# A conv block on one core: the map's 3x3 convolution by a minimal algorithm F(4,3), with its rows staged in fours

## The reference, cut to what matters

```python
x = x + layer(group_norm(x))               # 32 groups
# layer(v):
res = conv3x3(v, W_id, b_id)               # all 8 images
cA, cH, cV, cD = swt2_level3(v[0])         # image 0: circular 8-tap filters,
                                           # dilations 1, 2, 4, rows and columns
low_att  = attention(cA, ...)              # 1x1 conv times a sigmoid scale per channel
high_att = attention(concat(cH, cV, cD))   # 64 -> 192 channels
dmt = concat([low_att, high_att])          # 256 channels
out = leaky_relu(conv3x3(dmt, W_enc, b_enc), 0.01)   # one image: "the map", for all 8
return out + res
```

## Time and profile before

| | us |
|---|---|
| median of 3 runs | 2208.15 (2202.99 to 2209.74) |
| the profiled execution: its time | 2206.73 |
| its span (first to last instruction) | 2204.9 |
| busy: PE / DVE / POOL / ACT | 2132.9 / 1435.6 / 878.9 / 823.5 |
| granted clock of PE, mean | 0.98 |

### The profile page before, as it was taken

One profiled execution on the slowest core, in us unless ns is written; L12 is line 12 of the kernel. 1 busy time (PEld: TensorE's weight loads), 2 busy tenths in 40 slices (PEclk: granted clock), 3 DMA queues, 4 the chain that ended last, 5 costly groups with the idle time before them and its releaser, 6 DMA issues.

```text
span 2204.9 us, 74566 instructions
## 1 busy us (share of the span) xinstructions
PE 2132.9 (97%) x33526; PEld 1521.1 (69%) x33526; DVE 1435.6 (65%) x2235; ACT 823.5 (37%) x765; POOL 878.9 (40%) x543
## 2 busy tenths in 40 slices
PE   8997799999999999997999999999999999999998
PEld 7894566666666666664767776677677876677776
DVE  6755455555555555522777777777777777777776
ACT  3432333333333333322344344344444443444442
POOL 0001544444444444510444444444444444444444
PEclk9987899999999999998999999999999999999999
DMA  7942777777777777603687787887888878878874
GB/s 182 307 148 84 193 166 162 166 164 164 166 164 164 165 163 163 139 2 83 172 202 196 201 208 196 203 206 199 206 206 200 205 200 206 203 197 205 206 196 141
DMA packets 109191, 391.38 MB, mean 178 GB/s; under 512 B 45513, under 2 KB 46056, under 8 KB 95144
## 3 DMA queue, kind: packets, MB, share of 16 engines
q1 hardware_dynamic: 108904, 386.89, 70.3%
HBM read 258.37 MB, written 128.45 MB: 175 GB/s over the span
## 4 chain that ended last, share of the span: by engine, by line
issue 30%; POOL 23%; POOLq 1%; DVE 0%; PE 0%
POOL stage L1172 23%; POOLq L1170 1%; PE ps L1151 0%; POOLq L1165 0%; DVE dev L1107 0%; DVE gsum L1111 0%; DVE quad L1101 0%; DVE gsum L1104 0%; DVE dev L1110 0%; DVE dev L1109 0%; DVE quad L1103 0%; DVE gvar L1112 0%; DVE gmean L1105 0%; POOL root L1164 0%; POOLq L1163 0%
## 5 line engine op out<-in xcount | busy, mean ns | idle before, releaser
L1172 POOL TENSOR_TENSOR stage<-stage,big 128x448 f32<-128x448 f32 x448 | 511.1, 1141 | 661.5 <-DVE stage L1078 661.5
L1078 DVE SCALAR_TENSOR_TENSOR stage<-ps,w_max,xs 64x448 f32<-64x448 f32 x832 | 568.2, 683 | 79.3 <-PE ps L1146 55.0
L1146 PE MATMUL ps<-x_hi,w_hi 64*64 64x448 f16 x8064 | 454.0, 351 | 18.2 <-issue 18.0
L1036 ACT ACTIVATE x_hi<-xs,norm_now 128x2240 f16<-128x2240 f32 x104 | 234.9, 2258 | 608.5 <-PE ps L1146 605.8
L1146 PE MATMUL ps<-x_hi,w_lo 64*64 64x448 f16 x8064 | 451.0, 350 | 0.1
L1146 PEld LDWEIGHTS ps<-x_hi,w_hi 64*64 64x64 f16 x8064 | 294.8, 107 | 125.0 <-issue 23.5
L1146 PEld LDWEIGHTS ps<-x_hi,w_lo 64*64 64x64 f16 x8064 | 294.6, 107 | 106.0 <-issue 3.4
L810 PE MATMUL ps<-d_odd,shared 128*64 128x448 f16 x3024 | 293.5, 353 | 0.0
L810 PE MATMUL ps<-pool_of,shared 128*64 128x448 f16 x3024 | 293.5, 353 | 0.0
L916 DVE SCALAR_TENSOR_TENSOR big<-ps,e_max,lin 128x448 f32<-128x448 f32 x56 | 38.3, 683 | 331.0 <-ACT lin L869 331.0
L810 PEld LDWEIGHTS ps<-d_odd,shared 128*64 128x64 f16 x3024 | 172.4, 109 | 114.6
(11 more groups left out here) (176 smaller groups left out, 1739.7 us busy)
## 6 DMA issues: line engine op xcount, KB each, us to landing
xs<-in_x SPq DMA_DIRECT2D x200, 560.0 KB, 7.1
out<-stage SPq DMA_DIRECT2D x448, 224.0 KB, 3.1
big<-in_x SPq DMA_DIRECT2D x196, 448.0 KB, 7.4
row_filtered<-big SPq DMA_DIRECT2D x4, 6272.0 KB, 21.4
pool_of<-row_filtered SPq DMA_DIRECT2D x54, 448.0 KB, 9.9
pool_of<-in_x SPq DMA_DIRECT2D x32, 392.0 KB, 6.7
big<-in_x SPq DMA_DIRECT2D x8, 560.0 KB, 7.3
xs<-in_x SPq DMA_DIRECT2D x8, 504.0 KB, 7.3
```

What stands on the lines that cost most here:

```text
L1036: act.activation(x_hi[p][:, :, 1:1 + W], xs[slot][:, :].rearrange("p (r w) -> p r w", w=W), ACT.Identity, scale=scale, bias=bias).then_inc ...
L1078: dve.scalar_tensor_tensor(stage[p][o, r, g, :], psum[4 * p + 2 * g + r][o, 0:NT], w_max[lanes, 0:1], xs[slot][lanes, c:c + NT], ALU.mult, ...
L1146: mm = pe.matmul(psum[4 * p + 2 * g + r][C * k:C * k + C, 0:NT], w[lanes, t, :], v[lanes, y:y + 2, kx:kx + W], start=(j == 0), stop=(j == ...
L1172: pool.tensor_tensor(stage[p][:, r, g, :], stage[p][:, r, g, :], e_map[:, e:e + NT], ALU.add)\
```

## The change

The map's convolution is computed along a row by the minimal algorithm F(4,3): four neighbouring outputs need six products (at the points 0, 0.75, -0.75, 1.5, -1.5 and infinity) instead of twelve. The input transform is linear along the row, so it is multiplied into the column filter's matrices `fw`: a generated tile now holds for each of 56 groups of four columns six transformed values (2 x 336 = 672 columns instead of 448, in two PSUM banks). The weights are transformed on DVE. The output transform is made of sums and scalings of the six products on DVE, POOL and ACT, and the leaky ReLU is now x + relu(99 x), the result scaled. Rows come in fours: 56 loads of 4 rows instead of 28 of 8.

PE's tiles and convolution:

```diff
-                    if tile >= 4:
-                        pe.wait_ge(lo_done, tile - 3)
-                    for wc in (1, 0):            # 9 matmuls: 322, 126, 196 columns, 3 each
-                        ...
+                    if tile >= 2:
+                        pe.wait_ge(lo_done, tile - 1)
+                    for sw in range(2):          # 9 matmuls each: 246, 90, 168 columns
+                        o = psum[2 * (tile % 2) + sw][:, 0:VW]
+                        ...
+                    for place, i in enumerate(pair):      # pair of products
+                        o = [psum[bank][C*s:C*s+C, MN*place:MN*place+MN] for s in range(2)]   # MN = 224
+                        pieces = [(a, b, sw, ky) ...]     # 3 * 2 * 3 = 18
+                        for k, (a, b, sw, ky) in enumerate(pieces):
+                            for s in range(2):
+                                r = 4 * s + ky
+                                pe.matmul(o[s], weff[a][:, sw, i, ky, :],
+                                          d[n][:, b, r:r + 4, sw, NTILE*i:NTILE*i+NTILE], ...)
+                        if biased: ...                    # products 0, 1, 2, 5: two more
                 for step in range(NE):
                     for k in range(fresh(step)):
+                        u = 2 * step + 2 + k // CH
+                        if k % CH == 0:
+                            pe.wait_ge(s_split, u - 1)
+                        gen(tile_of(step, k), s_hl[u % 2][:, :, k % CH, :, :])
...
+                    conv(step, 5, (1, 2))
+                    conv(step, 6, (3, 4)).then_inc(conv_done, 1)
+                    if step:
+                        pe.wait_ge(z_done, step)
+                    conv(step, 4, (0, 5)).then_inc(conv_done, 1)
```

SP (load(u) waits for s_split of u - 3, that is until the rows before last are split):

```diff
-                for step in range(NE):
-                    u = step + 2
-                    ...
-                        load(u)
-                    for k in range(CPS * step, min(CPS * step + CPS, NCK)):
-                        load_stats(k)
+                for k in range(2):
+                    load_stats(k)
+                for step in range(NE):
+                    for u in (2 * step + 4, 2 * step + 5):
+                        if u < NU:
+                            load(u)
+                    for k in range(CPS * step + 2, min(CPS * step + 2 + CPS, NCK)):
+                        load_stats(k)
```

DVE in a step (stat(j) is one statistics instruction, four are a chunk):

```diff
+                    now = 16 * (step - 1)
                     for k in range(fresh(step)):
                         lo(tile_of(step, k), m, 2 + k)
-                    for q in range(2): ...        # take_stats twice, then the max
+                        if step and k % 2 == 1:
+                            stat(now)
+                            now += 1
+                        if step and k == 4:
+                            outer(step - 1)       # z0, z3 += products 0, 5
+                    while step and now < 16 * step:
+                        stat(now)
+                        now += 1
+                    pairs(step)                   # sums and differences of products 1 to 4
```

POOL and ACT in a step:

```diff
+                for step in range(NE):            # POOL
+                    if step:
+                        inner(step - 1)           # four additions of 224 elements
+                    for u in (2 * step + 4, 2 * step + 5):
+                        if u < NU:
+                            normal_rows(u)        # waits for the rows' DMA
+                        if step and u % 2 == 0:
+                            leaky(step - 1)       # one addition of 896 elements
+                    for u in (2 * step + 4, 2 * step + 5):
+                        if u < NU:
+                            split_lo(u)
...
+                    if step:                      # ACT
+                        act.wait_ge(conv_done, 2 * step)
+                        scale(step - 1)           # three copies of 224 elements
+                    for k in range(fresh(step)):
+                        hi(tile_of(step, k), m, 2 + k)
+                        if step and k == 5:
+                            positive(step - 1)    # relu(99 z), 896 elements
...                                               # the carried rows, now 2688 elements
+                    split_hi(2 * step + 4)
+                    put(step - 1)                 # waits for leaky; four of 224 elements
+                    split_hi(2 * step + 5)
+                    copy_second(step)             # products 2 and 4, before pairs
```

```diff
                 for k in range(FIRST):            # ACT
                     hi(k, 0, 1 + k)
-                split_hi(1)
+                    if k == 1:
+                        act.activation(weff[0]..., u32..., ACT.Identity, scale=einv[:, 0:1])
+                    if k == 5:
+                        split_hi(2)
+                split_hi(3)
...
+                    if k == 1:                    # DVE, behind lo(1)
+                        dve.wait_ge(weights_high, 1)
+                        dve.scalar_tensor_tensor(weff[1]..., u32..., einv[:, 0:1], weff[0]..., ...)
...
+                pool.wait_ge(weights_ready, 1)    # POOL
+                for u in (2, 3):
+                    normal_rows(u)
+                    split_lo(u)
```

More of the change, by code:

```diff
@@ L747, in tile_of, with rows_of, part_of, z_of @@
             return FIRST + ER * step + k
+        def rows_of(u):
+            return CH - 1 if u == NU - 1 else CH
+        def part_of(n):
+            v = e_map[:, n * EN:(n + 1) * EN] if n < NE else early[:, (n - NE) * EN:(n - NE + 1) * EN]
+            return v.rearrange("p (k n) -> p k n", k=4)
+        def z_of(step):
+            return part_of(step + 2)
+        def side_of(step):
+            return part_of(step + 3)
+        LATE = (ROWS - 2 * SX) // EN
         with nc.Block() as block:
@@ new lines, in gen, with add_bias @@
+                    mm.then_inc(gen_done, 1)
+                def add_bias(o, i, row):
+                    j, v = (0, 1, 2, None, None, 3)[i], 1 if i == NI - 1 else 0
+                    parts = [(0, 1, 0), (1, 4, 1)] if row == 0 else [(0, 3, 1), (3, 4, 2)] if row == H - 4 else [(0, 4, 1)]
+                    for a, b, kind in parts:
+                        m = inside[:, kind:kind + 1, v, :].broadcast_to((P, b - a, NTILE))
+                        mm = pe.matmul(o[:, a * NTILE:b * NTILE], bw[:, j, :], m, start=False, stop=(b == 4))
+                    return mm
@@ new lines, in conv @@
+                def conv(step, bank, pair):
+                    n = step % 2
+                    for place, i in enumerate(pair):
+                        o = [psum[bank][C * s:C * s + C, MN * place:MN * place + MN] for s in range(2)]
+                        pieces = [(a, b, sw, ky) for a, b in ((0, 0), (0, 1), (1, 0)) for sw in range(2) for ky in range(3)]
+                        biased = i not in (3, 4)
+                        for k, (a, b, sw, ky) in enumerate(pieces):
+                            for s in range(2):
+                                r = 4 * s + ky
+                                mm = pe.matmul(o[s], weff[a][:, sw, i, ky, :], d[n][:, b, r:r + 4, sw, NTILE * i:NTILE * i + NTILE],
+                                               start=(k == 0), stop=(k == len(pieces) - 1 and not biased))
+                        if biased:
+                            for s in range(2):
+                                mm = add_bias(o[s], i, ER * step + 4 * s)
+                    return mm
@@ L849, in _, with put @@
-                act.wait_ge(pads_set, 7)
+                    act.wait_ge(s_ready, u - 1)
+                    act.wait_ge(gen_done, CH * (u - 1) + 1)
+                    act.copy(s_hl[u % 2][:, :, :, 0, :].rearrange("w h r e -> w (h r) e"),
+                             s_in[u % 2].rearrange("w h r e -> w (h r) e")).then_inc(s_high, 1)
+                def put(step):
+                    act.wait_ge(leaky_done, step + 1)
+                    o = e_map[:, step * EN:(step + 1) * EN].rearrange("p (n k) -> p k n", k=4)
+                    for k in range(4):
+                        ins = act.activation(o[:, k, :], z_of(step)[:, k, :], ACT.Identity, scale=e_max[:, k:k + 1], bias=b_id[:, 0:1])
+                    ins.then_inc(map_done, 1)
@@ new lines, in scale @@
+                def scale(step):
+                    act.wait_ge(ab_done, step + 1)
+                    if step == LATE - 4:
+                        act.wait_ge(rows_out[1], 32)
+                    if step == NE - 3:
+                        act.wait_ge(stat_used, NCK)
+                    if step:
+                        act.wait_ge(leaky_done, step)
+                    side = side_of(step)
+                    for k in (3, 1, 2):
+                        ins = act.activation(side[:, k, :], ab[:, k % 2, 1, :], ACT.Copy, scale=2.0 ** k)
+                    ins.then_inc(scaled, 1)
```

597 lines of the change are left out of this document (361 added, 236 removed).

## The result

| | before | after |
|---|---|---|
| median | 2207.59 us (4 runs, 2202.99 to 2209.74) | 2763.47 us (4 runs, 2760.01 to 2764.24) |
| ratio | | 1.2518 [1.2496, 1.2541] |
| the profiled execution: time, span | 2206.73, 2204.9 | 2762.81, 2761.0 |
| mean granted clock of PE | 0.98 | 0.87 |

The account below looks back on a forecast made before the run. PE bounded the old kernel; a 51.5 us ring of waits would bound the new map. 249.9 + 1233.4 (ring steps) + 66.4 + 1183.1, plus 1.8, gave 2734.6, adjusted to the median 2736 us; range 2500 to 2880.

Parts of the forecast that it names:

- g: Moment in a map step when its generated tiles may start; the predicted period runs from one to the next, 51.5 us.
- T1: Moment when DVE ends a step's statistics and SP's last chunk wait ends; predicted at g + 29.3 us.
- the ring: In map steps: tiles, statistics, row request, POOL's row work, next tiles, without the convolution; 51.5 us a step instead of 28.0.
- Step 1 (17.6): From g to the step's first statistics chunk (a) used up: 17.6 us, 14.8 without the slow clock.
- Step 2 (11.7): From chunk a used to T1: refilling and using the step's remaining statistics chunks (b, c, d), 11.7 us.
- Step 3 (8.1): From T1 to the rows landed, behind the rest of one chunk and another chunk in the queue: 8.1 us.
- Step 4 (14.1): POOL's chain from landed rows to the next g: normalisations, leaky addition, split and semaphores, 14.1 us.
- Before the map: Stretch ahead of the map's steps: tiles start at 206, convolution 0 at 239 (before 251.9), ending at 249.9.
- Behind step 25: After that map step: last tiles 12, two convolutions 21.8, tail 5.6, then 1183.1 us to the end.
- PE as the bound (2074): Rival for the map: rows and chunks always there, a step is PE's 24 us, 2074 us in all; 7%.
- Chunks pacing the step (2239): Rival for the map: statistics chunks, not rows, pace each step, 30.6 us, 2239 in all; 7%.
- The clock that stays down in the tiles (2866): Rival for the map's tiles: short PE waits keep them at 1.2 GHz, 130 us more, 2866 in all; 8%.

Follow-up runs that it names:

- experiment 1: Changed kernel with each step's statistics chunk requests shifted four chunks earlier, so row requests no longer stand behind a wait for that step's statistics: 2249.31 us, ratio 1.0178 to before.
- experiment 3: Changed kernel with every product's convolution matmuls issued twice: 2830.82 us (one run).
- 9: Kernel of experiment 2 with each product's matmuls issued twice: 2394.74 us (one run).
- experiments 5: Changed kernel with 136 unread matmuls of 448 columns behind the convolution in steps 1 to 26, to keep PE's clock up: 2777.00 us, ratio 1.2568 to before.
- experiment 6: Changed kernel with 136 unread matmuls of 448 columns behind the convolutions of steps 1 to 24 only: 2728.95 us (one run).
- experiment 7: Changed kernel with POOL's leaky addition moved from between the two normalisations to ahead of the wait for the rows: 2726.06 us, ratio 1.2318 to before.
- experiment 8: Kernel of experiment 2 with one more statistics instruction behind tiles 1 and 4: 2097.45 us, ratio 0.9485 to the kernel before.
- experiment 10: Kernel before the change with only the two large sigmoid-scale multiplications moved from DVE to ACT: 2199.78 us, ratio 0.9951.
- experiment 2: Kernel of experiment 1 with a statistics instruction behind every tile instead of every second one: 2120.28 us, ratio 0.9582 to the kernel before.
- experiment 11: Kernel before the change with all sigmoid-scale multiplications, the bias's two included, moved from DVE to ACT: 2195.54 us, ratio 0.9945.

## Why the prediction was right, step by step

The terms, in the profiled execution:

| | forecast | measured |
|---|---|---|
| first tile | 206 | 200.9 |
| convolution 0, start and end | 239, 249.9 | 241.4, 252.3 |
| g to chunk a used | 17.6 | 17.0 |
| to T1 | 11.7 | 13.0 |
| to rows landed | 8.1 | 8.5 |
| POOL, to the next g | 14.1 | 13.7 |
| period | 51.5 | 52.3 |
| 24 periods | 1233.4 | 1255.0 |
| step 25 | 27 | 25.2 |
| last tiles, two convolutions, tail | 39.4 | 42.4 |
| to the end | 1183.1 | 1186.1 |
| sum | 2732.8 | 2761.0 |

The forecast is 1% under the result, and 22 of the 28 us are the ring. That it is so near is in part luck: of the ring's four steps two were taken too long and two too short. One by one:

- **The mechanism** held. SP's written order puts the row request behind a wait that ends with DVE's last statistics; experiment 1 turns that one thing round and gets 514 us back. That the convolution is outside the ring is shown by experiment 3 (1.1 of 10.9 us seen a period) against 9 (9.9 of 10.9).
- **Step 1 (17.6)** was 0.6 too much. The tiles were sized rightly (a pair of tiles 3.26 us, forecast 3.3; in ACT's casts 729.81 to 733.07), and so was the slow start: two tiles in 5.0, forecast 5.2. But the price of the clock, 17.6 against 14.8, was given as 2.8, and experiments 5 and 6 measured 15.0 with a warm clock, 2.0 less than 17.0, and 1.4 to 1.5 for the whole period. At full clock the pairs of tiles wait for the turn of PE, ACT and DVE, which may be why the slow PE costs less than its own columns say; that was not tested. At full clock a matmul of 90 columns and one of 168, with a load of 128 columns each, came every 0.12 us, 60 ns a piece, and a tile took 1.38, forecast 1.35. The rule of the Trainium skill that was weighed ("TensorE: Matmul & The Clock Gate", Back-to-back issue gap), some 81 ns per load and matmul, isn't borne out here.
- **Step 2 (11.7)** was the mis-sized term, 1.3 too little. The rate was not the error. It was taken as 238 GB/s, and once the data flow the window shows 235:

```profile
738.50:740.50 2.00, 2.00 (x48) 2.00 (x44) 2.00 (x4) 0.88 (x1) 0.00 (x0) 1.00 0.41 90
740.50:745.20 4.70, 4.70 (x104) 4.70 (x100) 0.11 (x2) 0.00 (x0) 0.00 (x0) 1.00 1.02 235
```

Over the 24 periods chunk d lands 4.0 us behind chunk c (median), as in the sum (23.1 to 27.1). But chunk c lands 6.7 behind the use of chunk a, where the sum had 5.5 (17.6 to 23.1). So what was too small is the time from SP's two requests until the data flow, which the sum took as 1.3 with no row to show it: the 6.7 less the 4.0 of a whole chunk leave some 2.7 (an estimate). Behind the requests of 738.49 the first two microseconds ran at 90 GB/s, and DVE waited 4.59 and 1.95 us for chunks c and d.

- **Step 3 (8.1)** was 8.5. In the period shown SP issues the last chunk's two DMAs and then the rows 1.2 us behind T1, and these land 7.3 later.
- **Step 4 (14.1)** was 13.7: 4 x 2.35, 2.07 and the first split's 2.1, as sized; experiment 7 shows that even the small leaky addition in it is paid.

**Before the map** two errors cancelled. The tiles began 5 us earlier than forecast: DVE's new weight work did not become the last there, and the gap ahead of the tiles was 3.07 instead of 8.84. But convolution 0 began 2.4 later. The second group of tiles waited 4.88 us for DVE's bias chain, which the sum did not have: its first instruction, 6x256 elements, took 2.38 us, as it began under a POOL instruction and ended with it:

```profile
226.94 0.79 PE L937 MATMUL ps<-pool_of 112*128 112x246 f16 x3 [4.88 <-DVE pool_of L1124]
...
223.62 2.38 DVE L1119 TENSOR_SCALAR big<-big,einv 6x256 f32<-6x256 f32 x1
...
223.52 2.34 POOL L252 TENSOR_TENSOR pool_of<-pool_of 112x1024 f32<-112x1024 f32 x1
```

It looks like the same stall as in the earlier trace rows, which the change removed in one place and made in another. The Trainium skill ("SBUF — State Buffer", Who interferes with whom) tells of a pair of ports that DVE and GpSimd share and that the first to issue keeps for its whole instruction; on DVE's side that concerns an instruction with two inputs from SBUF, and a `tensor_scalar` (a scaling) whose operands allow a faster mode. The traces agree: L602, L1119 (scalings) and L607 (two inputs) were held until POOL's instruction ended, while DVE's copies from PSUM ran under POOL's in 0.48 to 0.62 us and its statistics, with one input from SBUF, in 0.61.

**Behind step 25** the sum was 6.0 us short. The last put of the map ended 9.4 us behind the last convolution (1565.5 to 1574.9), not 5.6: ACT's scaling (0.95 us) and POOL's additions (1.88) also stand in that chain, and ACT's put took 2.41 where the prediction has 4 x 0.35. From there to the end it was 1186.1 instead of 1183.1, in a main stage that was not changed.

**The rivals.** PE as the bound (2074) could only come without the ring; experiment 8 is that case at 2097. Chunks pacing the step (2239) is experiment 1, 2249. The clock that stays down in the tiles (2866) did not come: tiles 0.3 us apart ran at full clock in every version, and in experiment 8 the window over 25 steps reads 1.00. So in the changed kernel's ring the clock is down behind the long idle of each period and not between tiles, and experiment 6 gives its price. Shorter pauses can bring it down too (last section).

## What to carry to other kernels

When loads of different urgency share one in-order queue, look for the request that stands behind a wait on work of the same step: here it closed a ring of 52 us around a step whose busiest engine had 24 us of work, and a faster algorithm made the kernel 25% slower. Follow each request from the instruction that frees its buffer to the one that needs its data, and count the whole path, latencies included; if it comes back to the same step, halving the work of an engine outside it brings nothing. Put the urgent load first and spread the consumer of the other over the step: the same algorithm then was 5% faster than the kernel before.

## What the hardware showed that was not expected

- Short pauses brought the clock down, but not each time. After 2.48 us of idle in experiment 10 PE ran at full clock for about a microsecond and then at half from 176 to 189; after 3.07 us ahead of the changed kernel's first tile (200.92) half a tile took 1.32 us until 206, against 0.70 at full clock, and after another 3.09 us, at 212.71, the clock fell again for some 3 us. Pauses of 0.54 us and the many of 0.3 between tiles did not. In between, experiment 2 shows both: behind PE pauses of 1.82, 2.33, 2.46, 2.93 and 3.07 us (ending at 355.5, 583.8, 816.2, 611.5 and 788.9) the clock fell some 1.0 to 1.4 us after work went on, for 3.4 us each time, and behind pauses of 1.68 and 2.71 us (ending at 557.7 and 432.7) it did not. So the length of the pause alone does not decide.
- A DVE product of 64x1 elements can take 4.23 us, when it starts under POOL's long instruction (experiment 10). Its size did not matter: 64x64 elements took 4.40. Taking the instruction away from DVE helped (experiment 11).
- Doubling the matmuls of a step delayed the rows' landing by 1.0 us, and filling it with others by 0.3. What they have in common with a transfer was not settled.
